# A graph layer pair on one core: scaled aggregates, PSUM inputs and a last stage on x1+message rows

## The reference

```
deg  = in-degree + 1;  dinv = deg ** -0.5
agg  = segment_sum((x @ W)[src] * dinv[src] * dinv[dst], dst) + (x @ W) * dinv**2 + b
x1   = layernorm(x + leaky_relu(agg, 0.01))                        # rows
r    = concat(x1[src], x1[dst], edge) @ Wr.T + br
q, k, v = x1 @ Wq.T + bq, r @ Wk.T + bk, r @ Wv.T + bv             # 8 heads of 64
attn = softmax of (q[dst] . k) / 8 over the edges of one dst, per head
y    = x1 + segment_sum(v * attn, dst) @ Wo.T + bo
y    = (y - mean) * rsqrt(var + eps) * gamma + beta                # mean, var over the nodes
out  = layernorm(x1 + y)                                           # rows
```

## Time and profile before

| | us |
|---|---|
| median of 3 runs (1659.83 to 1660.71) | 1660.66 |
| the profiled execution | 1665.52 |
| its span | 1663.4 |
| PE busy | 1390.4 (84%) |
| VectorE busy | 1235.9 (74%) |
| POOL busy | 1111.2 (67%) |
| ScalarE busy | 553.6 (33%) |
| node stage, about | 253 to 612 |
| edge stage, about | 612 to 1387 |
| last stage, about | 1387 to 1663 |

### The profile page before, as it was taken

How to read it: one execution, slowest core, us unless ns; L and a number is a source line. 1 busy time by engine, 2 the same in 40 slices (tenths; PEclk the granted TensorE clock), 3 DMA queues, 4 the chain that set the end, 5 groups by cost and what they waited for, 6 DMA issues and landing times. The chain is left out here.

```text
span 1663.4 us, 26922 instructions
## 1 busy us (share of the span) xinstructions
PE 1390.4 (84%) x7928; PEld 1140.6 (69%) x7928; DVE 1235.9 (74%) x2017; ACT 553.6 (33%) x996; POOL 1111.2 (67%) x1146
## 2 busy tenths in 40 slices
PE   1888895888888839999999999999999934767766
PEld 1888894666666629999999999999999832333332
DVE  4545544999999952778788888788888775766666
ACT  1555551444444421322222232222322111333333
POOL 3766625777777733467767777777777556777775
PEclk9999997999999969999999999999999966999999
DMA  4778644666666632334554334553344424776775
GB/s 126 221 237 265 217 176 148 190 189 189 189 189 189 190 105 86 111 107 133 149 165 114 114 127 126 146 172 114 114 127 125 121 71 127 255 235 235 233 239 185
DMA packets 123981, 272.39 MB, mean 164 GB/s; under 512 B 19504, under 2 KB 19952, under 8 KB 123808
## 3 DMA queue, kind: packets, MB, share of 16 engines
q1 hardware_dynamic: 93472, 176.89, 32.8%
q0 software_dynamic: 29920, 93.89, 19.0%
q10 hardware_dynamic: 544, 1.05, 0.2%
HBM read 198.22 MB, written 73.61 MB: 163 GB/s over the span
## 5 line engine op out<-in xcount | busy, mean ns | idle before, releaser
L159 PE MATMUL pse<-w_lo,w_hi 128*128 128x256 f32 (+1 forms) x1440 | 466.2, 324 | 24.6 <-DVE w_lo L1051 21.1
L161 PE MATMUL pse<-w_hi 128*128 128x256 f32 (+1 forms) x1440 | 461.8, 321 | 0.0
L160 PE MATMUL pse<-w_hi,w_lo 128*128 128x256 f32 (+1 forms) x1440 | 461.8, 321 | 0.0
L159 PEld LDWEIGHTS pse<-w_lo,w_hi 128*128 128x128 f32 x1440 | 277.0, 192 | 44.9 <-issue 23.7
L161 PEld LDWEIGHTS pse<-w_hi 128*128 128x128 f32 x1440 | 276.7, 192 | 19.8
L160 PEld LDWEIGHTS pse<-w_hi,w_lo 128*128 128x128 f32 x1440 | 277.2, 193 | 18.7
L895 POOL TENSOR_TENSOR acc_x<-acc_x,node_rows 128x512 f32<-128x512 f32 (+1 forms) x79 | 129.9, 1644 | 94.3 <-DMA node_rows<-x_table 89.6
L1291 PE MATMUL psf<-fin_x,ident 128*128 128x512 f32 x158 | 88.1, 640 | 70.2 <-POOL fin_x L1261 65.5
L159 PE MATMUL psn<-w_lo,agg_hi 128*128 128x512 f32 x316 | 133.8, 423 | 2.9 <-DVE agg_lo L713 2.9
L160 PE MATMUL psn<-w_hi,agg_lo 128*128 128x512 f32 x316 | 126.6, 401 | 0.0
L161 PE MATMUL psn<-w_hi,agg_hi 128*128 128x512 f32 x316 | 126.5, 400 | 0.0
(11 more groups left out here) (191 smaller groups left out, 3287.0 us busy)
## 6 DMA issues: line engine op xcount, KB each, us to landing
coef_all<-coef_table SPq DMA_DIRECT2D x40, 512.0 KB
node_x<-in_x SPq DMA_DIRECT2D x79, 256.0 KB
x_table<-node_x SPq DMA_DIRECT2D x79, 256.0 KB, 2.1
node_rows<-x_table SPq DMA_DIRECT2D x79, 256.0 KB
fin_x<-x_table SPq DMA_DIRECT2D x79, 256.0 KB
out_dram<-fin_y SPq DMA_DIRECT2D x78, 256.0 KB, 2.1
edge_part<-part SPq DMA_DIRECT2D x20, 512.0 KB
sum_table<-sums SPq DMA_DIRECT2D x40, 256.0 KB
```

The source lines that it names most:

```text
L159: pe.matmul(to, left[0], right[1], start=first, stop=False)
L160: pe.matmul(to, left[1], right[0], start=False, stop=False)
L161: return pe.matmul(to, left[0], right[0], start=False, stop=last)
```

## The change

- Aggregation: POOL's program is written out without a loop and takes the indices straight from `edge_idx`, which has a fifth column (the destination's place in the dinv table). A fourth gather per tile brings `dinv_dst`, and ScalarE multiplies the summed rows by it when it copies them out of PSUM. The index stage also makes `dinv_sq`.
- Node stage: VectorE forms `dinv_sq * x + sum` for all tiles, last in its step. The product then needs no factor, and b enters PSUM by a matmul of a ones matrix with a two-row tile. ScalarE copies the product to z, and the leaky step takes PSUM and z. x1 and y have four slots. PE's product is of tile j-4 in step j (was j-3), and the lags behind it grow.
- Edge stage: VectorE makes x1+message rows from PSUM and the gathered x1 rows, which are what is stored in `msg_table`. Of a message tile it adds the messages to `sum_y`; ScalarE squares the x1+message rows into PSUM and the gathered x1 rows in place; VectorE adds the first squares to `acc_xx`, POOL the second to `sum_xx`, which is subtracted at the end.
- Last stage: ScalarE copies x1 of a tile to u. POOL's gather overwrites the rows of nodes that have edges and skips the others (by a bound on the index). VectorE multiplies u by scale, and PE adds shift (one matmul), x1 as loaded and u. POOL scales nothing. SP's step j loads tile j and then stores tile j-7.
- The last factor of the shift in the row statistics is now a `tensor_scalar` with two scalars.

```diff
 aggregation, POOL
-    nc.gpsimd.tensor_copy(idx[:, s, :], g.edge_idx[...]).then_inc(idx_ok, 1)
-    wait_alone(pool, idx_ok, t + 1, g.passed)
-    for i, (to, of, n) in enumerate(((ea_rows, g.ea, ea_in), (x_rows, g.x, x_in), (dinv_src, g.dinv_table, x_in))):
...
+    rows_of(g.ea, ea_rows[:, s, :], t, 0).then_inc(ea_in[s], 16)
+    wait(pool, scaled_ok, t - R + 1)
+    rows_of(g.x, x_rows[:, s, :], t, 1).then_inc(x_in[s], 16)
+    rows_of(g.dinv_table, dinv_src[:, s, :], t, 2).then_inc(x_in[s], 16)
+    rows_of(g.dinv_table, dinv_dst[:, t, :], t, 4).then_inc(x_in[s], 16)
 aggregation, ScalarE
-    nc.scalar.copy(sums[:, q, :], ps_back[q][:]).then_inc(row_ok, 1)
+    nc.scalar.activation(sums[:, q, :], ps_back[q][:], ACT.Copy, scale=dinv_dst[...]).then_inc(row_ok, 1)
 node stage, SP
-    if on(7):
-        sp.wait_ge(x1_ok, j - 6)
+    if on(9):
+        q = (s - 9) % RY
+        sp.wait_ge(x1_ok, j - 8)
...
 node stage, POOL
+    for j in range(NT + 7):
+        if j >= 7:
+            i = j - 7
+            pool.wait_ge(leaky_ok, i + 1)
+            wait(pool, x1_ok, i - RY + 1)
+            nc.gpsimd.tensor_tensor(y[:, i % RY, :], z[:, i % 2, :], xr[:, i % RX, :], ALU.add).then_inc(y_ok, 1)
+        if j < NT:
+            wait(pool, agg_ok, j - RS + 1)
+            nc.gpsimd.indirect_dma_start(out=rn[:, j % RS, :], ..., in_=g.sum_table, ...).then_inc(rn_in[j % RS], 16)
 node stage, ScalarE, in this order in a step
+    if on(6):
+        act.wait_ge(mm_ok, j - 5)
+        wait(act, y_ok, j - 7)
+        nc.scalar.copy(z[:, q, :], ps_o[(s - 6) % 4][:]).then_inc(z_ok, 1)
+    if on(3):
+        h = (s - 3) % 2
+        act.wait_ge(turned, j - 2)
+        wait(act, mm_ok, j - 4)
+        nc.scalar.copy(g_hi[:, h, :, :], by_k(ps_t[h][:])).then_inc(hi_ok, 1)
+    if on(9):
+        act.wait_ge(scale_ok, 2 * (j - 9) + 2)
+        wait(act, x1_out[q], landed(j, s, 9 + RY, RY))
+        nc.scalar.activation(x1[:, q, :], y[:, q, :], ACT.Identity, bias=..., scale=...).then_inc(x1_ok, 1)
+    if on(8):
+        act.wait_ge(stat_ok, 2 * (j - 8) + 2)
+        nc.scalar.activation(root[:, h, :], mv[:, h, 1:2], ACT.Sqrt, bias=g.eps[:]).then_inc(root_ok, 1)
 node stage, VectorE, in this order in a step
+    if on(6):
+        dve.wait_ge(z_ok, j - 5)
+        v.scalar_tensor_tensor(z[:, q, :], ps_o[(s - 6) % 4][:], NEG_SLOPE, z[:, q, :], ALU.mult, ALU.max).then_inc(leaky_ok, 1)
+    if on(3):
+        dve.wait_ge(hi_ok, j - 2)
+        v.tensor_tensor(g_lo[:, h, :, :], by_k(ps_t[h][:]), g_hi[:, h, :, :].bitcast(F32), ALU.subtract).then_inc(lo_ok, 1)
+    if on(8): bn_stats of y
+    if on(9): reciprocal
+    if on(8): bn_aggr
+    if on(9): tensor_scalar for the shift
+    if on(2):
+        dve.wait_ge(x_in[(s - 2) % RX], landed(j, s, 2, RX))
+        dve.wait_ge(rn_in[(s - 2) % RS], landed(j, s, 2, RS))
+        wait(dve, turned, j - 3)
+        v.scalar_tensor_tensor(gr[:, h, :], xr[...], g.dinv_sq[:, bass.ds(j - 2, 1)], rn[...], ALU.mult, ALU.add).then_inc(agg_ok, 1)
 node stage, PE, in this order in a step
     if on(2):
-        wait_agg(pe, j - 2, s)
+        pe.wait_ge(agg_ok, j - 1)
         wait(pe, lo_ok, j - 3)
...
-    if on(3):
-        pe.wait_ge(lo_ok, j - 2)
-        wait(pe, z_ok, j - 6)
+    if on(4):
+        pe.wait_ge(lo_ok, j - 3)
+        wait(pe, leaky_ok, j - 7)
+        pe.matmul(to, ones_r[:], b_two[:], start=True, stop=False)
...
 edge stage, VectorE; it stands ahead of sums_of_v in the step
+    if on(4):
+        for q in range(2):
+            dve.wait_ge(o_mm, t + 1)
+            dve.wait_ge(again_in[q], 16 * (j - 4) + 16)
...
+            v.scalar_tensor_tensor(both[:, q, :], ps_o[q][:], last, again[:, q, :], ALU.mult, ALU.add).then_inc(u_ok, 1)
+            wait(dve, m_added, t)
+            v.scalar_tensor_tensor(g.sum_y[:], ps_o[q][:], last, g.sum_y[:], ALU.mult, ALU.add).then_inc(m_added, 1)
...
+    if on(4):
+        for q in range(2):
+            dve.wait_ge(uu_ok, t + 1)
+            v.tensor_tensor(g.acc_xx[:], g.acc_xx[:], ps_o[q][:], ALU.add).then_inc(uu_added, 1)
 edge stage, ScalarE
+            nc.scalar.activation(ps_o[q][:], both[:, q, :], ACT.Square).then_inc(uu_ok, 1)
+            nc.scalar.activation(again[:, q, :], again[:, q, :], ACT.Square).then_inc(xx_ok, 1)
-            nc.scalar.activation(msg[:, q, :], ps_o[q][:], ACT.Copy, scale=g.is_last[...]).then_inc(msg_ok, 1)
 edge stage, POOL: three operations on a message tile become one
+            nc.gpsimd.tensor_tensor(g.sum_xx[:], g.sum_xx[:], again[:, q, :], ALU.add).then_inc(xx_added, 1)
 edge stage, PE: turn_scores and messages wait for uu_added in place of msg_ok
 last stage, SP
-    if on(5):
-        sp.wait_ge(norm_ok, j - 4)
+    if on(7):
+        q = (s - 7) % RY
+        sp.wait_ge(norm_ok, j - 6)
...
 last stage, POOL
+    for j in range(NT):
+        pool.wait_ge(u_ok, j + 1)
+        nc.gpsimd.indirect_dma_start(out=u[:, q, :], ..., in_=g.msg_table, ..., bounds_check=EP - 1, oob_is_err=False).then_inc(u_in[q], 16)
 last stage, ScalarE; three copies come ahead of the stage's square root
+    def copy(j, s):
+        act.wait_ge(x_in[s], x_before[s] + landed(j, s, 0, R))
+        wait(act, sum_ok, j - R + 1)
+        nc.scalar.copy(u[:, s, :], x1[:, s, :]).then_inc(u_ok, 1)
+    if on(1) and not (isinstance(j, int) and j - 1 < AHEAD): copy(j - 1, (s - 1) % R)
+    if on(6): root
+    if on(7): normalised rows
 last stage, VectorE in this order: u * scale of j-5, reciprocal of j-7, bn_stats of j-6, shift of j-7, bn_aggr of j-6
 last stage, PE: the sum of j-5
+    pe.matmul(to, ones_r[:], shift[:], start=True, stop=False)
+    pe.matmul(to, g.ident[:], x1[:, q, :], start=False, stop=False)
+    pe.matmul(to, g.ident[:], u[:, q, :], start=False, stop=True).then_inc(sum_ok, 1)
```

More of the change, by code:

```diff
@@ L384, in _ @@
                 v.tensor_copy(g.edge_idx[:, :, 3], cols_s[:, 0, :])
+                v.scalar_tensor_tensor(g.edge_idx[:, :, 4], low[:, 0, :], float(NT), high[:, 0, :], ALU.mult, ALU.add)
                 dve.wait_ge(hist_ok, 1)
@@ L601, in node_stage, with by_k @@
             "node_z_ok", "node_leaky", "node_y_ok", "node_stat", "node_root_ok", "node_scale", "x1_ok"))
-        x1_out = [sem(f"x1_out{s}") for s in range(2)]
+        x1_out = [sem(f"x1_out{s}") for s in range(RY)]
         def by_k(row):
             return row.rearrange("p (k e) -> p k e", k=K)
[L607 to L612, removed]
+        def by_k(row):
+            return row.rearrange("p (k e) -> p k e", k=K)
         with nc.Block() as block:
@@ L655, in _ @@
+                for acc in (g.acc_x, g.acc_xx, g.sum_y, g.sum_xx):
                     nc.gpsimd.memset(acc[:], 0.0)
@@ L735, in step @@
                         for k in range(K):
-                            mm = g.product(pe, ps_o[(s - 3) % 4][:], [h[:, q, k, :] for h in (g_hi, g_lo)],
-                                           [g.w(h, W0, k) for h in (g.w_hi, g.w_lo)], k == 0, k == K - 1)
+                            mm = g.product(pe, to, [h[:, q, k, :] for h in (g_hi, g_lo)],
+                                           [g.w(h, W0, k) for h in (g.w_hi, g.w_lo)], False, k == K - 1)
                         mm.then_inc(mm_ok, 1)
-                sweep(pe, NT, 3, 8, 8, step)
+                sweep(pe, NT, 4, 8, 8, step)
@@ L909, in step @@
                             t = 2 * (j - 3) + q
-                            wait(pool, added, 2 * (t - 2) + 2)
+                            wait(pool, xx_added, t - 1)
                             nc.gpsimd.tensor_copy(idx2[:, q, :], g.edge_idx[:, bass.ds(t, 1), 3]).then_inc(again_idx, 1)
@@ L1303, in step @@
                 def step(j, s, on):
-                    if on(4):
+                    if on(1) and not (isinstance(j, int) and j - 1 < AHEAD):
+                        copy(j - 1, (s - 1) % R)
+                    if on(6):
                         h = s % 2
-                        act.wait_ge(stat_ok, 2 * (j - 4) + 2)
+                        act.wait_ge(stat_ok, 2 * (j - 6) + 2)
                         nc.scalar.activation(root[:, h, :], mv[:, h, 1:2], ACT.Sqrt, bias=g.eps[:]).then_inc(root_ok, 1)
-                    if on(5):
-                        h, q = (s - 5) % 2, (s - 5) % RY
-                        act.wait_ge(scale_ok, 2 * (j - 5) + 2)
-                        wait(act, y_out[q], landed(j, s, 9, RY))
+                    if on(7):
+                        h, q = (s - 7) % 2, (s - 7) % RY
+                        act.wait_ge(scale_ok, 2 * (j - 7) + 2)
+                        wait(act, y_out[q], landed(j, s, 7 + RY, RY))
                         nc.scalar.activation(y[:, q, :], ps_y[q][:], ACT.Identity, bias=mv[:, h, 3:4], scale=mv[:, h, 2:3]).then_inc(norm_ok, 1)
-                sweep(act, NT, 5, 8, 16, step)
+                sweep(act, NT, 7, 8, 16, step)
             @block.vector
```

327 lines of the change are left out of this document (142 added, 185 removed).

## The result

The kernel after took 1900.4 us (median of four runs, 1894.2 to 1905.0), the kernel before 1660.7 beside it. The ratio is 1.143, 95% interval 1.138 to 1.148.

| stage | before, us | after, us | difference | forecast |
|---|---|---|---|---|
| aggregation (from 31) | 221.8 | 229.7 | +8 | +10 |
| node | 358.2 | 630.5 | +272 | +301 |
| edge | 774.4 | 767.9 | -6.5 | -8 |
| last | 278.0 | 238.0 | -40 | +2 |

What follows compares the result with a forecast made beforehand. Limits before: POOL's queue in aggregation, VectorE most in the node stage, PE in the edge stage, no full engine last. Terms +300 + 1 + 0 + 2 + 10 - 8 = +305 on 1665.5 give 1970, as median 1965 us; range 1840 to 2100.

Steps and rivals of the forecast that it cites:

- A loop closes: Node stage: transposes, older product, high copy and VectorE's steps wait for each other in turn, spanning one tile; +300 us.
- The loop's length, 7.9 us: Node stage: time a tile, 7.9 us against 4.10 before; bounds 6.7 at full clock and 9.8 at the lower.
- The lower clock: Node stage: PE's idle gaps slow its matmuls from 0.23 to 0.43 us apart, making a 6.7 us loop 8.3.
- three of four: Node stage: share of PE's bursts taken to be hit by slower matmuls, giving 7.9 us a tile.
- Last stage, 0 us: Last stage: a load becomes the bound at 3.33 us a tile against 3.23; 253 against 251.6 us, taken as 0.
- The round: Last stage: normalised rows, load issued and landed, copy, root, normalised rows; 6.66 us for two tiles.
- the landing: Last stage: time from a load's issue until its data is there, taken as 4.25 us from the node stage.
- loads land as fast as outputs: Rival, 10%: last-stage loads land in 2.1 to 2.6 us, stage loses 59 to 77 us, time about 1900.
- Aggregation, +10: Aggregation: a fourth gather replaces the index copy and its wait in POOL's queue; 0 to +22 us, taken as +10.
- The bare pace: Aggregation: POOL's time a tile without other waits, 4.46 us before and 5.0 after; at most +22 us.
- Edge stage, -8: Edge stage: PE hides the steady part; POOL's lighter work shortens the 11.7 us after the last product to 4.1; -8 us.
- the signs named: Expected profile: node tiles 7 to 8.5 us apart, PE half busy, clock under 0.95, last stage 3.2 to 3.4 a tile.

Runs made afterwards that it cites:

- either half of the old order: Two variants of the kernel after: TensorE's product put ahead of the transposes, 1602.0 us; or the product again that of tile i-1, transposes still first, 1603.5 us.
- dummy matmuls: The kernel after with 11 more 512-column matmuls behind each node-stage product, into a PSUM bank that nothing reads: 1836.5 us, ratio 1.111.
- third series: Later set of runs beside the kernel before: after unchanged 1.150, after without the fourth gather 1.127, before unchanged 0.999 of before.
- second series: Earlier set of runs beside the kernel before: after unchanged took 1966.3 us, ratio 1.176; after without the fourth gather 1.136.
- early sum: The kernel after with VectorE's weighted sum in the node stage moved up, right behind the low parts: 1829.2 us, ratio 1.106.

## Why the prediction was right, and where its sizes were off

- **"A loop closes".** Right, and shown in both directions: either half of the old order opens it (3.91 and 3.92 us a tile), and the tail moved out of it shortens it (6.76). The order, not the operations, makes the 272 us: with TensorE's order turned round the same operations take 3.91 us a tile, less than before's 4.10.
- **The loop's length, 7.9 us.** Measured 7.65. At full clock it is 6.84 (dummy matmuls) where the sum of rows gave 6.7. VectorE's tail was priced too low: from statistics to weighted sum it takes 1.23 us (502.88 to 504.11), and the prediction has 0.98. The lower clock costs 0.81, where I had taken 1.2. A loop that meets it is 8.4 us, or 1.5 longer (forecast 8.3, or 1.6 longer), but 44 of 76 bursts meet it, not three of four. That gaps bring the lower level is right (the granted clock is 0.87 with them and 1.00 with matmuls in them). How often was a guess: no run shows the three of four behind the 7.9. Its reason ("every gap now exceeds the one that did it") means the 1.83 us before the burst at 412.02, in which the granted clock was 0.50 from 413.5 to 416.5 us. That such a gap is always enough is not shown: after gaps of 3.2 us 32 of 76 bursts kept the full clock. The loop as a whole made the stage 20 us too long in the forecast (79 x 0.25), after two errors that partly cancel; the other 9 of the stage's 29 lie in its first and last tiles.
- **Last stage, 0 us.** The round is right: ScalarE's copy waits for a load issued two tiles back. The mis-sized term is the landing. I took 4.25 us from the node stage of before. There it is usual (median 4.0 in the third series), but the loads of the last stage land in 3.4 us, before the change and after it. With 3.4 the round is 5.8, or 2.9 us a tile; measured 2.70. Part of the rest is that on ScalarE an instruction starts before the one ahead of it has ended: from copy to normalised rows it is 0.72 us (1784.00 to 1784.72), where I had 0.87. The stage makes 42 of the 71 us between the two sums. What sets a landing stays open. Within after's last stage it rose with the traffic: 3.4 us at 211 GB/s, 3.75 at 261, 4.24 at 266 with one more load under way. But before's loads took 4.0 us in the node stage at 180 GB/s (250 to 560 us) and 3.4 in the last stage at 232 (1395 to 1645 us, third series). The rival "loads land as fast as outputs", to which I gave 10%, was half true: 40 of its 59 to 77 us came. No run shows its 2.6 us, and the 59 us that go with it, for a load of the last stage: there the loads landed in a median of 3.4 at 203 GB/s. A median of 2.6 is that of the same size of load in after's node stage, at 98 GB/s.
- **Aggregation, +10.** Near by the first profile (+8), but by luck: the profile of before had 13 us of stalls in this stage. Between two kernels on one chip without stalls it is +21, nearly the upper bound of 22. The bare pace held +50 for the gather (1.25 x 40) and -28 for the index copy and its wait (1.96 - 1.25, x 40); measured are +40, and -20 for the rest of the change. That one chip adds 41 us with three gathers and 64 with four was not foreseen and would not be from this profile.
- **Edge stage, -8.** Measured -6.5, and the tail makes all of it: the last product ended at 1653.9, POOL's last sum at 1657.8, 4.0 us against 11.7 (forecast 4.1). The "nothing" for the steady part fits, but no experiment isolated it.
- **The time.** 1900 is also the time that the prediction gave for fast loads alone. That is partly chance: 29 of the 71 us come from the node stage, which that rival left as it was. Of the signs named, the node tiles, the half-busy PE, the clock and the shorter tail came; 3.2 to 3.4 us a tile in the last stage did not (2.70).

## What to carry to other kernels

When an edit reorders one engine's queue, write down for each buffer slot which instruction frees it and whether that now stands behind the instruction that needs it; here a closed loop of hand-overs cost 7.65 us a tile, and no operation off TensorE in it lasts over 0.75. The loop here left TensorE idle, and then the lower clock cost once more, 0.81 of 7.65 us. Price a transfer's landing from many instances in the stage where it will run: the same size of load took 2.6, 3.4 and 4.0 us in three stages here. And when two rings have the same length, opening one may give nothing.

## What the runs showed of the hardware

- A fourth gather of 128 four-byte elements costs POOL's queue as much as one of 256 KB: 1.04 us of the engine and 0.3 before it, against 0.97 and 0.3 (means, after, third series).
- On the chip of the second series the aggregation of after ran 64 us longer than in its two other profiles, with idle times of 0.15 to 1.18 us between the matmuls of a product in the rows shown. With three gathers it lost 41 us against the third series (267.6 and 227.0). Between the two series the kernel before differed by 18 us in all. What held the instructions back the traces don't show; it stays open.
- Gaps of 2.1 us in every loop left TensorE at a granted clock of 0.83, gaps of 3.2 us at 0.87 (early sum and after). Putting 11 matmuls into each of the 79 gaps brought it to 1.00 and made the kernel 3% faster than after, with more work done.
